# Attention and two layers on one core: value product in the middle of a step, first-pass units reordered, seams between stages rewritten

## What is computed

```python
mod = (_silu(L0_c) @ L0_wmod).reshape(8, 6, 1, -1)
sa, ca, ga, sb, cb, gb = ...            # ga, gb kept away from zero
h = _layernorm(x) * (1 + ca) + sa
x = x + ga * attention(h, Wq, bq, Wk, bk, Wv, bv, Wp, bp)   # softmax(q k / 4 + causal mask) v, then Wp
h = _layernorm(x) * (1 + cb) + sb
x = x + gb * ffn(h)
# ffn: two times _layer(x):
#   qkv of shifted tokens, l2-normalised q and k times q_scale, k_scale, rotary tables (cos, sin, scale),
#   softmax over a window of 128 and the one before, @ wo, layer norm, a * gelu(g) with w1, w2
```

## Time and profile before

| | |
|---|---|
| median of three runs | 5578.67 us |
| lowest, highest | 5578.08, 5596.92 us |
| the profiled execution | 5582.27 us (span of the profile 5580.5) |
| mean granted clock | 0.876 |
| busy share of the span: PE, PEld, DVE, ACT, POOL | 79%, 57%, 59%, 47%, 34% |
| attention, by the first and last rows | 30.94 to 1729 us (store of f issued at 1728.80) |
| layer 0, layer 1 | 1744 to 3640 us, 3650 to 5574 us |
| chain that ended last: issue, POOL, PE, ACT, DVE | 16%, 8%, 7%, 1%, 1% |
| largest groups | L1487 POOL 533.9 us, L968 DVE 724.6, L637 ACT 603.6, L1590 ACT 498.7 |

### The profile page before, as it was taken

One profiled execution on the slowest core, in us unless ns is written; L12 is line 12 of the kernel. 1 busy time (PEld: TensorE's weight loads), 2 busy tenths in 40 slices (PEclk: granted clock), 3 DMA queues, 4 the chain that ended last, 5 costly groups with the idle time before them and its releaser, 6 DMA issues. The chain is left out here.

```text
span 5580.5 us, 99747 instructions
## 1 busy us (share of the span) xinstructions
PE 4388.4 (79%) x33294; PEld 3169.1 (57%) x33294; DVE 3284.6 (59%) x7520; ACT 2599.3 (47%) x5522; POOL 1905.4 (34%) x1485
## 2 busy tenths in 40 slices
PE   2888888888883878878778888758878788787886
PEld 1444444444443666666666666646666666666665
DVE  2665566556553755756657566555657556575564
ACT  0344444444453544545445454444545445454453
POOL 3122231221323433434334333334434344343443
PEclk6788888899896999989899899879899999999988
DMA  4324424333412000000000000010000000000000
GB/s 102 82 38 93 101 66 71 94 88 51 93 39 62 11 15 14 11 15 11 13 16 11 13 13 11 15 56 17 16 20 16 19 17 19 20 14 20 17 19 18
DMA packets 155749, 200.46 MB, mean 36 GB/s; under 512 B 29900, under 2 KB 130728, under 8 KB 155184
## 3 DMA queue, kind: packets, MB, share of 16 engines
q1 hardware_dynamic: 151088, 192.13, 14.3%
q10 hardware_dynamic: 4096, 1.06, 0.1%
HBM read 116.02 MB, written 67.68 MB: 33 GB/s over the span
## 5 line engine op out<-in xcount | busy, mean ns | idle before, releaser
L1487 POOL TENSOR_TENSOR b_e<-b_e,b_share 128x512 f32<-128x512 f32 (+1 forms) x512 | 533.9, 1043 | 1283.2 <-DVE b_share L1915 1283.2
L968 DVE TENSOR_REDUCE a_mx<-a_ring 128x2 f32<-128x1024 f32 (+3 forms) x768 | 724.6, 955 | 327.9 <-PE a_ring L789 203.9
L637 ACT ACTIVATE a_e_t<-a_ring 128x1024 f32<-128x1024 f32 (+3 forms) x768 | 603.6, 809 | 621.1 <-PE a_ring L789 392.8
L1590 ACT ACTIVATE b_e<-b_e,b_bias 128x256 f32<-128x256 f32 (+1 forms) x1024 | 498.7, 488 | 616.1 <-DVE b_bias L1895 614.8
L1693 PE MATMUL b_bank_m<-b_h_t_hi,b_w_hi 128*128 128x256 f32 x1584 | 475.5, 300 | 99.7 <-POOL b_h_t_lo L1493 76.2
L1693 PE MATMUL b_bank_p<-b_wqkv_hi,b_turned_hi 128*128 128x512 f32 x768 | 369.5, 481 | 184.2 <-ACT b_qk L1562 140.6
L802 PE MATMUL a_ring<-a_k_st,a_q_st 48*128 48x512 f32 (+3 forms) x1536 | 361.7, 469 | 146.3 <-ACT a_e_t L637 94.1
L1693 PE MATMUL b_bank_m<-b_h_t_lo,b_w_hi 128*128 128x256 f32 x1584 | 460.9, 291 | 0.0
L1693 PE MATMUL b_bank_m<-b_h_t_hi,b_w_lo 128*128 128x256 f32 x1584 | 459.8, 290 | 0.0
L827 PE MATMUL a_ring<-a_q_st,a_k_st 50*128 50x512 f32 (+3 forms) x1536 | 362.6, 471 | 108.6 <-DVE a_qk_p L947 64.2
L1895 DVE CUSTOM_DVE_ANT_0 b_e<-b_bank_s,b_mask,b_scale_q 128x256 f32<-128x256 f32 (+1 forms) x1024 | 433.5, 459 | 0.7
(11 more groups left out here) (220 smaller groups left out, 11074.1 us busy)
## 6 DMA issues: line engine op xcount, KB each, us to landing
a_q_st<-a_parts_q SPq DMA_DIRECT2D x192, 128.0 KB, 4.4
a_k_st<-a_parts_k SPq DMA_DIRECT2D x192, 128.0 KB, 7.4
b_fl<-f_rows SPq DMA_DIRECT2D x72, 256.0 KB, 4.0
a_parts_q<-a_qk_p SPq DMA_DIRECT2D x16, 1024.0 KB, 9.4
a_parts_k<-a_qk_p SPq DMA_DIRECT2D x16, 1024.0 KB, 4.0
a_xl<-in_L_attn_x SPq DMA_DIRECT2D x9, 1024.0 KB, 9.2
f_rows<-b_fr SPq DMA_DIRECT2D x33, 256.0 KB, 2.3
b_x_l<-x_rows SPq DMA_DIRECT2D x33, 256.0 KB, 3.7
```

Source lines behind the costliest of these rows:

```text
L637: act.activation(e_t[:, step % 2, 2 * pair:2 * pair + 2, 0:cols], slot[:, :].rearrange("p (h t) -> p h t", h=2)[:, :, 0:cols], ACT.Exp).th ...
L968: dve.reduce_max(mx[:, g % 2, :, pair, piece, t:t + 1], slot[:, :].rearrange("p (r c) -> p r c", r=2)[:, :, 0:cols], AX.X)\
L1487: pool.tensor_tensor(weights, weights, share[:, pp, :].unsqueeze(2) .broadcast_to([P, 2, 2 * WIN - lo]), ALU.mult).then_inc(e_done.sem, 1)
L1590: ins = act.activation(weights, weights, ACT.Exp, scale=-1.0, bias=bias[:, pp, hh:hh + 1], accum_out=total[:, pp, hh:hh + 1])
```

## The change

1. `clear` and `prime` deal the semaphores out to five engines, `sems[0::5]` and so on, each in its own block.
2. In an attention step the value product of the step before (with `turn_output`) stands between the first unit and scores 1, no longer behind the second unit. ScalarE and VectorE keep their order.
3. The first pass has another order of units: `UNIT_AT` replaces `UNIT_T`. By steps n = 0 to 11, four steps ahead of the scores, the unit columns were 512, 384, 384, 512, 256, 512, 512, 128, 128, 512, 512, 256 and are 512, 512, 256, 128, 512, 512, 384, 512, 256, 512, 384, 128. The score columns are 512, 384, 256, 128, five times 512, 384, 256, 128.
4. Attention's lead: x(0) is normalised, scaled and shifted on VectorE; its statistics come first, the weights' low part after; x(1) is loaded behind the first stacks, and its statistics are inside the first pass. Waits on the low part and on the constants stand at their use.
5. Attention's closing: VectorE adds the second half of x1, takes all statistics and modulates six of eight tiles, GpSimd two.
6. Layers: the rotary tables are stored so that each partition's part is contiguous; the scales have a semaphore of their own with the tables (`tab_loaded`), the second half of the f loads comes behind the tables, and the waits of ScalarE, TensorE and VectorE on low parts, small vectors and tables stand at the first use, in the first step of the body.

```diff
 
     with nc.Block() as block:
+        @block.sync
+        def _(sp):
+            for s in sems[0::NENG]:
+                sp.sem_clear(s)
+
         @block.gpsimd
         def _(pool):
-            for s in sems:
+            for s in sems[1::NENG]:
                 pool.sem_clear(s)
+
+        @block.scalar
...
-UNIT_T = (0, 7, 1, 6, 2, 5, 3, 4)
-UNITS = [(t, piece, pair) for t in UNIT_T for piece in range(t // 4 + 1) for pair in range(2)]
+UNIT_AT = ((5, 1), (3, 0), (2, 0), (0, 0), (5, 0), (4, 0), (1, 0), (4, 1), (7, 1), (7, 0), (6, 1), (6, 0))
+UNITS = [(t, piece, pair) for t, piece in UNIT_AT for pair in range(2)]
...
-            for half in range(CK):
-                store_parts(2 * half, 0)
-                store_parts(2 * half + 1, 0)
-                load_stacks(2 * half, 0)
+            store_parts(0, 0)
+            store_parts(1, 0)
+            load_stacks(0, 0)
             load_x(1, 1)
+            store_parts(2, 0)
+            store_parts(3, 0)
             load_stacks(1, 0)
+            load_stacks(2, 0)
             load_stacks(LAST, 0)
...
-            modulate_x(0)
+            pool.sem_inc(x_scaled.sem, 2)
+            pool.sem_inc(x_scaling.sem, 1)
             modulate_x(1)
...
                 pool.wait_ge(biased.sem, biased.at(i, 1))
-                for p in range(2):
+                for p in range(1 if closing else 2):
                     pool.wait_ge(gated.sem, gated.at(i, 2 * p + 2))
                     half = slice(4 * p, 4 * p + 4)
                     pool.tensor_tensor(x1[:, half, :], x1[:, half, :], f_t[:, half, :], ALU.add)\
                         .then_inc(x1_done.sem, 1)
-                modulate(f_t, x1, "f", modb[:, 1:2, :], modb[:, 2:3, :], f_scaling, f_scaled, f_done, i)
+                if closing:
+                    rows, shape = f_t[:, END:TB, :], [P, TB - END, C]
+                    pool.wait_ge(end_scaled, 1)
+                    pool.tensor_tensor(rows, rows, modb[:, 2:3, :].broadcast_to(shape), ALU.mult)\
+                        .then_inc(end_scaled, 1)
+                    pool.wait_ge(end_scaled, 2)
+                    pool.tensor_tensor(rows, rows, modb[:, 1:2, :].broadcast_to(shape), ALU.add).then_inc(end_done, 1)
+                else:
+                    modulate(f_t, x1, "f", modb[:, 1:2, :], modb[:, 2:3, :], f_scaling, f_scaled, f_done, i)
...
-                        scores(g, n, 1, a)
-                        for group, k, at in units[1:]:
-                            first_pass(group, k, at)
                         if n > 0:
                             meet_values(g, n - 1, a)
                         elif mode != "lead":
...
                             turn_output((g - 1) % G1, 1, a - (g == 0), g, a)
                         if n == 5:
                             turn_output(g, 0, a, g, a)
+                        scores(g, n, 1, a)
+                        for group, k, at in units[1:]:
+                            first_pass(group, k, at)
                         if mode == "body":
                             for what in PREP_AT.get((g, n), []):
                                 prepare(what, i + 1)
...
                     x_statistics(0)
+                    dve.wait_ge(hi_split, 3)
+                    dve.tensor_tensor(w_lo[:, :, :, :], w_raw, w_hi[:, :, :, :].bitcast(F32), ALU.subtract)\
+                        .then_inc(lo_split, 1)
                     nearer("x", 0)
+                    dve.wait_ge(rstd_of["x"].sem, rstd_of["x"].at(0, 1))
+                    step(normalise(xl, xl, "x", range(TB)))
+                    dve.wait_ge(mod_in_loaded.sem, mod_in_loaded.at(0, 1))
+                    step(dve.tensor_tensor(xl[:, :, :], xl[:, :, :], mod_in[:, 1:2, :].broadcast_to([P, TB, C]),
+                                           ALU.mult))
+                    dve.tensor_tensor(xl[:, :, :], xl[:, :, :], mod_in[:, 0:1, :].broadcast_to([P, TB, C]),
+                                      ALU.add).then_inc(h_ready.sem, 1)
                     for c in range(CK):
                         low(("xT", c), xT_hi, 0)
                     for m in MATRICES:
                         for half in range(2):
                             qk_low(("qk", m, half), 0)
+                    dve.wait_ge(const_made, 16)
                     for q in range(4):
                         take_values(("v", q), 0)
-                    x_statistics(1)
-                    nearer("x", 1)
                     for k in range(NUNIT):
                         reduce_unit(0, k, 0)
+                        if k == NUNIT // 2:
+                            x_statistics(1)
+                        if k == NUNIT * 3 // 4:
+                            nearer("x", 1)
...
-                    x1_statistics(0, i)
-                    step(x1_statistics(1, i))
+                    dve.wait_ge(gated.sem, gated.at(i, 4))
+                    dve.wait_ge(biased.sem, biased.at(i, 1))
+                    dve.tensor_tensor(x1[:, 4:TB, :], x1[:, 4:TB, :], f_t[:, 4:TB, :], ALU.add)\
+                        .then_inc(x1_done.sem, 1)
+                    dve.wait_ge(x1_done.sem, x1_done.at(i, 2))
+                    step(statistics("f", x1, range(TB)))
                     variances("f")
                     nearer("f", i)
+                    dve.wait_ge(rstd_of["f"].sem, rstd_of["f"].at(i, 1))
+                    normalise(f_t, x1, "f", range(END, TB)).then_inc(end_scaled, 1)
+                    step(normalise(f_t, x1, "f", range(END)))
+                    step(dve.tensor_tensor(f_t[:, 0:END, :], f_t[:, 0:END, :],
+                                           modb[:, 2:3, :].broadcast_to([P, END, C]), ALU.mult))
+                    dve.tensor_tensor(f_t[:, 0:END, :], f_t[:, 0:END, :], modb[:, 1:2, :].broadcast_to([P, END, C]),
+                                      ALU.add).then_inc(end_done, 1)
...
-    return np.stack([cos * scale, sin * scale, cos / scale, sin / scale]).astype(f)
+    rows = np.stack([cos * scale, sin * scale, cos / scale, sin / scale]).astype(f)
+    return np.ascontiguousarray(rows.reshape(4, NWIN, P, D2).transpose(0, 2, 1, 3)).reshape(4, T, D2)
 
...
+            for u in range(NU // 2):
                 sp.dma_start(fl[:, blocks_of(u), :], rows_of(f_in, 0, u)).then_inc(f_loaded[u // 2].sem, 16)
-
+            sp.dma_start(qk_scale[:, 0, :], qs.partition_broadcast(P)).then_inc(tab_loaded, 16)
+            sp.dma_start(qk_scale[:, 1, :], ks.partition_broadcast(P)).then_inc(tab_loaded, 16)
             sp.wait_ge(stage_zero, 5)
             for n in range(CK):
...
             for n in range(4):
-                sp.dma_start(tab[:, n // 2, n % 2, :, :], tables[n].rearrange("(w p) d -> p w d", p=P))\
-                  .then_inc(small_loaded, 16)
-            sp.dma_start(qk_scale[:, 0, :], qs.partition_broadcast(P)).then_inc(small_loaded, 16)
-            sp.dma_start(qk_scale[:, 1, :], ks.partition_broadcast(P)).then_inc(small_loaded, 16)
+                sp.dma_start(tab[:, n // 2, n % 2, :, :], tables[n].rearrange("(p w) d -> p w d", p=P))\
+                  .then_inc(tab_loaded, 16)
+            for u in range(NU // 2, NU):
+                sp.dma_start(fl[:, blocks_of(u), :], rows_of(f_in, 0, u)).then_inc(f_loaded[u // 2].sem, 16)
             with nc.allow_non_contiguous_dma(reason="vectors that go one value to a partition"):
                 sp.dma_start(ln_g[:, :], lg.rearrange("(k p) -> p k", p=P)).then_inc(small_loaded, 16)
...
-            pool.wait_ge(small_loaded, 16 * NSMALL)
+            pool.wait_ge(tab_loaded, 16 * NTAB)
...
             act.wait_ge(const_made, n_const - 1)
-            act.wait_ge(lo_split, len(pieces))
-            act.wait_ge(small_loaded, 16 * NSMALL)
             act.preload_act_table_set("natural_log_exp_and_others")
...
                                     .then_inc(f_hi.sem, 1)
+                        if pp == FIRST:
+                            act.wait_ge(lo_split, len(pieces))
+                            act.wait_ge(small_loaded, 16 * NSMALL)
...
-            dve.wait_ge(small_loaded, 16 * NSMALL)
-            dve.wait_ge(tab_made, 4)
-            dve.wait_ge(const_made, n_const)
+            dve.wait_ge(const_made, n_const - 1)
...
                             split_f(int(pp == F_LATER))
+                        if pp == FIRST:
+                            dve.wait_ge(const_made, n_const)
+                            dve.wait_ge(tab_made, 4)
+                            dve.wait_ge(small_loaded, 16 * NSMALL)
                         if 0 <= pp < NPP:
                             scores_met(pp)
```

62 lines of the change are left out of this document (52 added, 10 removed).

## The result

The change took the median from 5579.47 to 5489.51 us (four runs each, 5470.39 to 5493.08 after); the ratio is 0.9827, with a 95% interval from 0.9805 to 0.9849. That is -90 us by the medians and -97 by the ratio, against -130 forecast (5448.5); it is faster by more than 0.5%, and inside the range. The profiled execution of the changed kernel took 5489.2 us (span 5487.4), 93 less than that of the kernel before.

What follows compares the result with a forecast made beforehand. No engine is full: attention is a ring of three PSUM slots with engines waiting in turn, and seams are chains. Seams -95, with the body -130, took 5582.3 to 5452; the median, 3.6 lower, gave 5448.5 us; range 5350 to 5500.

Steps and rivals of the forecast that it cites:

- Semaphores: Stage seams: SyncE's 33.0 us of waits for clears and priming fall to 9 with five engines sharing, -24 us.
- Lead, second half: Attention's lead: x(1) loaded earlier, its statistics amid the reductions, which end at 136 instead of 156 us, -20 us.
- rival that a transfer stays late: Leads: x(1) or the rotary tables land as late as before, 20 us lost, 5468 us; chance 0.12.
- Closing: Attention's closing: VectorE's new share of add, statistics and modulation ends sooner, -11 us (between -9 and -12).
- Attention body: Attention's steps: new step order and unit table together, -35 us, bounds +30 and -80 at an unchanged clock.
- (b): Attention body: wide first-pass units now beside wide scores, about 0.8 us a group over 31 groups, -25 us.
- (c): Attention body: a first block's value product waits for ScalarE's output copy behind one more exponential, +12 us.
- (a): Attention body: the value product fills the scores' wait for VectorE's split of q or k projections, -22 us.
- the cycle is turned by half a step: 0 for a full step: Attention body: the wait for exponentials leaves unit 1 but returns at the next unit 0, so no gain.
- the clock case: Rival, at attention's group changes: TensorE's clock stays up, saving 96 us more, 5352 us; chance 0.2.
- the slower mechanism: Rival, narrow scores beside narrow units: TensorE waits, its clock falls twice more a group, 248 us, 5696 us; chance 0.03.
- case that the body gives nothing: Rival, attention body: gains end in the transfer chain, or (c) equals (a) and (b), 5483 us; chance 0.25.

Runs made afterwards that it cites:

- spreading the issues: ScalarE's four DMAs of the next group's maxima issued singly over steps 9 to 11: 5529.32 us on the kernel before, 5404.25 us on the changed kernel.

## Why the forecast was right where it was, and where not

*Semaphores*, -24 forecast, about -16 measured (the three seams: 9.9 to 5.6, 15.4 to 9.2 and 12.6 to 6.8 us from the last store to the next stage's first DMA, 16.3 in all). The step that failed is the sum on SyncE's wait. The wait did shrink by 26, as the row suggested, but SyncE now works through a fifth itself, and the code says that this is no wait; what a seam costs is the time from store to first DMA, which I should have summed. What of the rest is barrier and what is a slower rate of the other engines isn't separated. The term itself had 0.3 us for each barrier, which no run shows.

*Attention lead, first half*, -20: -19.2. Tiles took 4.25 and not 3.4, beside GpSimd's masks, and that is the whole difference.

*Lead, second half*, -20: -22.5, and +4.0 behind it. The transfer of x was in time. The rival that a transfer stays late came true in a place that I had not looked at: 8 KB of maxima behind the stacks.

*Closing*, -11: -10.6 from gates to store. The price of the two engines' meeting did come, 2.0 us of the 2.3 allowed for, but VectorE paid it and not GpSimd; VectorE's tiles alone are 0.8 cheaper than in the sum, 0.33 from start to start. And in front of it the way from the last exponential to the add ran longer, 19.7 instead of 16.3 us, for the most part in a stretch at the lower clock. With that the closing's end is -7.2.

*Layer leads*, -20: -22 (-10.6 without the seam, and -11.4).

*Attention body*, -35: -9.3 in the profiled execution. (b), the units, -25: -18 alone, and by the trace more from the clock than from the idle time that I had summed. (c), the copy of the output, +12: the value product waits for it 2.4 us in all. (a), the projections' split, -22: the waits fell by 18.4, to 39.2 and not to under 15 as I had written, and groups 0 and 1 got shorter by more than that, 3.4 and 4.6 us a sample, 56 in seven samples, 1.5 a sample of it in group 1 from the units. The value product alone gave 3.7 and 3.5, 50 us, so this was too low rather than too high: the other steps of these groups gain too, and the chain of transfers absorbs only a part (the sixth step of group 1 went from 8.1 to 10.3 us, the fifth and tenth are 0.5 and 0.3 longer, all others of it are shorter). The step that failed is the line "the cycle is turned by half a step: 0 for a full step". It took the period of a full step at one clock for the whole price. What the turn costs is time at the lower clock, which I priced nowhere: behind step 9, where ScalarE is away for its issues, the clock falls in either order, but with the value product in the middle it stays down for 27 us in 8 or 9 of 14 cases, where it was 1, though the gap in front is much the same (1.56 us against 1.46 with the value product alone). And the clock case I had as a rival with only one sign: it could rise. It fell: 27 us stretches, and a closing at 0.65 instead of 0.93. I had the slower mechanism at the wrong place (narrow steps) with chance 0.03, and the right one, behind the issue queue, named only as the obstacle to a gain.

The rival of a clock that stays up (96 us for 24 changes of group) was not what the change does, but there is such a sum to be had: spreading the issues, which takes away half the falls, gave 51 us on the kernel before, for which the rival was written, and 72 to 85 on the changed kernel. The case that the body gives nothing (5483) is what came out by number, by another way than the one I gave: not absorbed by the transfer chain, but given back by the clock. So the time fell inside the range partly by luck: the range held that case, for a reason that isn't the one at work. The period of a sample went from 198.0 to 191.7 us, near the 193 that I had named, and says nothing of this, because the closing carried most of the loss.

What stays open: why the stretch at the lower clock lasts 13.7 us in one case and 27 in another with TensorE busy in both, and with gaps in front that don't differ. The runs show that the value product's place decides how often the long one comes, not by what.
